# Products of constants on PE inside the layer norm blocks of a twelve-sublayer transformer kernel

## The chip, the cores and the metric

The kernel runs on one core of a Trainium2 chip. The metric is device time in microseconds (us) of one execution. The engines are named as in the profile: PE (TensorE, its matmuls), PEld (TensorE's weight loads), DVE (VectorE), ACT (ScalarE), POOL (GpSimd) and SP (SyncE, which only issues DMAs here). PE's granted clock has two levels, 1.2 and 2.4 GHz, which the profile writes as 0.50 and 1.00.

## The reference

Four layers of three sublayers each (cross attention, self attention, feed forward) on x of 16 x 64 rows of 256 numbers, in float32. Each sublayer is added to x and begins with a layer norm of x:

```python
def _layernorm(x, axis=-1, eps=1e-05):
    m = jnp.mean(x, axis=axis, keepdims=True)
    v = jnp.var(x, axis=axis, keepdims=True)
    return (x - m) / jnp.sqrt(v + eps)
...
x = x + _L0_xattn_ref(_layernorm(x, axis=-1), ctx_1024, ctx_1024, ...)
x = x + _L0_attn_ref(_layernorm(x, axis=-1), ...)
x = x + _L0_ffn_ref(_layernorm(x, axis=-1), ...)
...
x = x + _L3_ffn_ref(_layernorm(x, axis=-1), ...)
```

So there are twelve of these norms. The cross attentions also read a context of 16 x 1601 rows of 256.

## The kernel before, in words

x stays in SBUF as 8 tiles (`T`) of 128 rows by 256 columns. `build` runs the twelve sublayers one after the other, each as a chain of blocks. A block gives each engine its own program; engines wait for each other by semaphores, the block ends when every engine's program has ended, and the helper `signals` (line 39) then clears the semaphores and puts a barrier of all engines behind it. So the next block starts when the slowest engine of this one has finished, SP's wait for its loads included.

Each sublayer begins with the helper `layernorm` (line 83). The twelve calls are, in order of time: `x0_ln` (line 573), `e0_in` (736), `f0_ln` (1199), `s1_ln` (1443), `a1_ln` (2214), `g1_ln` (2385), `x2_ln` (3633), `a2_ln` (3671), `f2_ln` (3976), `x3_ln` (4125), `a3_ln` (4350) and `q3_ln` (4415). In the texts they go by their first two letters: x0, e0, f0 and so on. Ten of them hand over `env.h_T`, in which the normed rows are wanted turned (features on the partitions); e0 and q3 hand over None and turn nothing.

Inside `layernorm`:

- DVE measures the 8 tiles (line 105) and gathers mean and variance per half of 4 tiles (line 110). ACT takes the square root (line 142), DVE inverts (line 115).
- ACT norms the 4 tiles of the first half (line 150), DVE those of the second half (line 129).
- PE turns each tile by two transposes of 128 x 128 (line 167) against the identity `env.ident`, 16 in all. It waits for each tile of the first half from ACT and for each of the second from DVE. The turned first half goes to PSUM banks 0 and 1, the second to 2 and 3.
- When a half is turned, ACT copies its one bank to `h_T` (line 155) and DVE its other (line 134). The semaphore `turned` tells them.
- SP issues the loads that the sublayer wants (line 72) and waits for them; those in `begun` (line 96, used by e0 and g1) are waited for only by who reads them.

The order on PE and in every queue is the order of the code; nothing is scheduled by a tool. What follows a norm differs: x0, x2, x3 go on with `linear_T` (line 265); s1 with 8 products at line 1457; a1 at line 2014; g1 at line 2458; a2 at line 3723; f0 and f2 with the experts' products at line 471, whose weights SP begins to load only in that next block (line 446); a3 with a small product at line 4376 whose input is loaded in the next block (line 4369).

`env.ident` is the first 128 columns of the tile `consts`, which is loaded once at the start and holds zeros, ones and some masks; it is wider than 512 columns. PSUM has 8 banks of 512 float32 columns; the norm uses banks 0 to 3.

Of the kernel before, what the change touches and what calls it, by code (L numbers as in the profile page):

```python
# [17 lines left out]
P = 128  # L18
# [6 lines left out]
NH = 512  # L25
# [57 lines left out]
def layernorm(nc, env, stage, src, nat, dst_T, loads=(), begun=(), begun_in=None):  # L83


    HALF = T // 2
    with signals(nc, stage, "loaded own stats std shift_ready rows_act rows_dve turned act_out "
                 "dve_out") as (
            loaded, own, stats, std_ready, shift_ready, rows_act, rows_dve, turned, act_out,
            dve_out):  # L90
        with nc.Block() as block:

            @block.sync
            def _(sp):
                for dst, src_rows in begun:
                    sp.dma_start(dst, src_rows).then_inc(begun_in, 16)
                load_all(sp, loads, loaded)

            @block.vector
            def _(dve):  # L100
                steps = Steps(dve, own)

                def measure(tiles):
                    for t in tiles:
                        steps.done(nc.vector.bn_stats(env.bn[:, t, :], src[:, t, :]))

                def aggregate(half):
                    steps.wait()
                    for t in range(HALF * half, HALF * (half + 1)):
                        nc.vector.bn_aggr(env.mv[:, t, :], env.bn[:, t, :]).then_inc(stats, 1)  # L110

                def invert(half):
                    ts = slice(HALF * half, HALF * (half + 1))
                    dve.wait_ge(std_ready, half + 1)
                    steps.done(nc.vector.reciprocal(env.rstd[:, ts], env.std[:, ts]))
                    steps.wait()

                measure(range(HALF))
                aggregate(0)
                measure(range(HALF, HALF + 1))  # L120
                invert(0)
                nc.vector.scalar_tensor_tensor(
                    out=env.shift[:, :], in0=env.mv[:, 0:HALF, 0], scalar=-1.0,
                    in1=env.rstd[:, 0:HALF], op0=ALU.mult, op1=ALU.mult).then_inc(shift_ready, 1)
                measure(range(HALF + 1, T))
                aggregate(1)
                invert(1)
                for t in range(HALF, T):
                    nc.vector.tensor_scalar(nat[:, t, :], src[:, t, :], env.mv[:, t, 0:1],
                                            env.rstd[:, t:t + 1], ALU.subtract,  # L130
                                            ALU.mult).then_inc(rows_dve, 1)
                for half in range(2 if dst_T is not None else 0):
                    dve.wait_ge(turned, 2 * half + 2)
                    nc.vector.tensor_copy(dst_T[:, 1, half * NH:(half + 1) * NH],
                                          env.ps[:, 2 * half + 1, :]).then_inc(dve_out, 1)

            @block.scalar
            def _(act):
                def deviations(half):
                    ts = slice(HALF * half, HALF * (half + 1))  # L140
                    act.wait_ge(stats, HALF * (half + 1))
                    nc.scalar.activation(env.std[:, ts], env.mv[:, ts, 1], ACT.Sqrt,
                                         bias=env.eps5[:, 0:1]).then_inc(std_ready, 1)

                deviations(0)
                act.wait_ge(shift_ready, 1)
                for t in range(HALF):
                    if t == HALF - 1:
                        deviations(1)
                    nc.scalar.activation(nat[:, t, :], src[:, t, :], ACT.Identity,  # L150
                                         scale=env.rstd[:, t:t + 1], bias=env.shift[:, t:t + 1]
                                         ).then_inc(rows_act, 1)
                for half in range(2 if dst_T is not None else 0):
                    act.wait_ge(turned, 2 * half + 1)
                    nc.scalar.copy(dst_T[:, 0, half * NH:(half + 1) * NH],
                                   env.ps[:, 2 * half, :]).then_inc(act_out, 1)

            @block.tensor
            def _(pe):
                for t in range(T if dst_T is not None else 0):  # L160
                    half, at = t // HALF, t % HALF * P
                    if half == 0:
                        pe.wait_ge(rows_act, t + 1)
                    else:
                        pe.wait_ge(rows_dve, t - HALF + 1)
                    for f in range(KT):
                        last = nc.tensor.transpose(env.ps[:, 2 * half + f, at:at + P],
                                                   nat[:, t, f * P:(f + 1) * P], env.ident)
                        if t % HALF == HALF - 1:
                            last.then_inc(turned, 1)  # L170

# [4358 lines left out]
def build(nc, d, out, where, names):  # L4532
    with ExitStack() as mem:
        def sb(name, shape, dt=F32):
            return mem.enter_context(nc.sbuf_tensor(name, shape, dt))

        env = Env()
        env.x = sb("x", [P, T, D])
        env.h = sb("h", [P, T, D])
        env.h_T = sb("h_T", [P, KT, N])  # L4540
        env.rows = sb("rows", [P, T, D])
        env.bn, env.mv = sb("bn", [P, T, 6]), sb("mv", [P, T, 2])
        env.std, env.rstd = sb("std", [P, T]), sb("rstd", [P, T])
        env.shift = sb("shift", [P, T // 2])
        consts = sb("consts", [P, d["consts"].shape[1]])
        env.ident = consts[:, where["ident"][0]:where["ident"][1]]
        env.ones = consts[:, where["ones"][0]:where["ones"][1]]
        env.same_head = consts[:, where["same_head"][0]:where["same_head"][1]]
        env.den_rows = consts[:, where["den_rows"][0]:where["den_rows"][1]]
        env.head_of = consts[:, where["head_of"][0]:where["head_of"][1]]  # L4550
        env.excluded = consts[:, where["excluded"][0]:where["excluded"][1]]
        env.parity = consts[:, where["parity"][0]:where["parity"][1]]
        env.iota8 = consts[:, where["iota8"][0]:where["iota8"][1]]
        env.valid_last = consts[:, where["valid_last"][0]:where["valid_last"][1]]
        env.cross = consts[:, where["cross"][0]:where["cross"][1]]
        env.own_state = consts[:, where["own_state"][0]:where["own_state"][1]]
        env.tenth = consts[:, where["tenth"][0]:where["tenth"][1]]
        env.block_of = consts[:, where["block_of"][0]:where["block_of"][1]]
        env.zero = consts[:, where["zero"][0]:where["zero"][1]]
        env.eps5 = consts[:, where["eps5"][0]:where["eps5"][1]]  # L4560
        env.eps6 = consts[:, where["eps6"][0]:where["eps6"][1]]
        env.minus1 = consts[:, where["minus1"][0]:where["minus1"][1]]
        env.state_mask = consts[:, where["same_head"][0]:where["head_of"][1]]
        env.ps = mem.enter_context(nc.psum_tensor("ps", [P, 8, NH], F32))

        with signals(nc, "start", "x_in consts_in") as (x_in, consts_in):
            with nc.Block() as block:

                @block.sync
                def _(sp):  # L4570
                    sp.dma_start(env.x[:, :, :], d["x"].rearrange("(t b) s n -> (b s) t n", b=2)
                                 ).then_inc(x_in, 16)
                    sp.dma_start(consts[:, :], d["consts"]).then_inc(consts_in, 16)
                    sp.wait_ge(x_in, 16)
                    sp.wait_ge(consts_in, 16)

        for name in names:
            SUBLAYERS[name](nc, env, d)

        with signals(nc, "end", "stored") as (stored,):  # L4580
            with nc.Block() as block:

                @block.sync
                def _(sp):
                    sp.dma_start(out.rearrange("(t b) s n -> (b s) t n", b=2), env.x[:, :, :]
                                 ).then_inc(stored, 16)
                    sp.wait_ge(stored, 16)
# [96 lines left out]
```

## Time and profile before

| what | value |
|---|---|
| time, median of 3 runs | 3715.51 us (3709.92 to 3716.82) |
| the profiled execution's own time | 3718.34 us |
| its span in the trace | 3716.5 us |
| mean granted clock of PE | 0.952 |
| PE busy | 3395.4 us, 91% of the span, 39440 products |
| DVE, ACT, POOL busy | 2017.8, 1690.3, 701.8 us |

The profiled execution took 3718.34 us, of which 3716.5 us lie inside the trace's span and 1.8 us around it. All times of rows are from the span's start. "Idle before" in a row of the timeline is how long the engine had done nothing when the work of that row began, and the name behind the arrow is what it waited for; "PEq" there stands for the queue of instructions itself, which is what a barrier between two blocks looks like. A matmul's record lasts from its start to its modelled end, so the records of successive products overlap; how far apart they start is what each costs in a row of them.

### The profile page before, as it was taken

How to read it: one execution, taken by the hardware profiler on the slowest of the kernel's cores; microseconds unless marked ns; L12 is line 12 of the kernel's file. 1: busy time of each engine (PE TensorE's matmuls, PEld its weight loads, DVE VectorE, ACT ScalarE, POOL GpSimd, SP SyncE). 2: the span in 40 equal slices, each digit the busy share in tenths (PEclk: the TensorE clock that was granted, in tenths of full speed). 3: DMA queues.
4: the chain of work that ended last, by engine and by line, in shares of the span. 5: the costliest groups of instructions: out<-in, count | busy, mean ns of one | idle time of the engine just before them, and what ended most of it. 6: DMA issues, size and time to landing. Idle time of an engine off the chain costs nothing. (4 is left out here: it accounts for less than half of the span.)

```text
span 3716.5 us, 90513 instructions
## 1 busy us (share of the span) xinstructions
PE 3395.4 (91%) x39440; PEld 2395.7 (64%) x39440; DVE 2017.8 (54%) x4042; ACT 1690.3 (45%) x3093; POOL 701.8 (19%) x343
## 2 busy tenths in 40 slices
PE   6999999779998979999879998999999789998975
PEld 4777777656675668888654455777776555554544
DVE  4666666654443267777546483565656443333337
ACT  3777777523332277887535452444444321111222
POOL 1776777311010000000122021101010000000001
PEclk8999999989999989999978998999999889999986
DMA  1111111021001415334010002111110013220710
GB/s 64 55 38 38 38 55 38 10 92 38 27 1 60 155 47 195 127 127 151 16 51 1 1 0 69 59 40 59 40 50 11 24 38 110 92 75 3 253 43 16
DMA packets 155253, 223.53 MB, mean 60 GB/s; under 512 B 39375, under 2 KB 134539, under 8 KB 154732
## 3 DMA queue, kind: packets, MB, share of 16 engines
q1 hardware_dynamic: 154860, 217.75, 17.6%
q8 instruction: 313, 5.13, 0.6%
q14 instruction: 80, 0.66, 0.1%
HBM read 216.67 MB, written 1.05 MB: 59 GB/s over the span
## 5 line engine op out<-in xcount | busy, mean ns | idle before, releaser
L3225 POOL TENSOR_TENSOR x_sc<-x_sc,h_T 128x2048 f32<-128x2048 f32 (+1 forms) x105 | 443.4, 4267 | 200.3 <-ACT h_T L3438 200.3
L3041 ACT ACTIVATE x_sc<-x_sc,x_nb 128x2048 f32<-128x2048 f32 (+1 forms) x112 | 210.6, 1880 | 297.6 <-DVE x_sc L3090 297.5
L3090 DVE SCALAR_TENSOR_TENSOR x_sc<-ps,x_nb,x_cap 128x2048 f32<-128x2048 f32 (+1 forms) x112 | 246.2, 2198 | 49.4 <-PE ps L2982 49.4
L3513 DVE TENSOR_TENSOR x_most<-x_most,ps 128x512 f32<-128x512 f32 (+1 forms) x352 | 234.8, 685 | 45.5 <-PE ps L3342 33.1
L1736 ACT ACTIVATE s1i_both<-ps,s_less,s_rs_s 128x64 f32<-128x64 f32 x624 | 215.2, 426 | 49.0 <-DVE s_less L1853 48.9
L3417 ACT COPY x_sc<-ps 128x1024 f32<-128x1024 f32 x192 | 179.4, 945 | 112.0 <-PE ps L3342 71.5
L3431 ACT ACTIVATE x_sc<-x_sc 128x2048 f32<-128x2048 f32 (+1 forms) x112 | 201.0, 1797 | 4.0 <-DVE x_sc L3225 3.9
L3298 PE MATMUL ps<-x_wv,x_ctx_T 128*128 128x256 f32 (+1 forms) x832 | 201.4, 383 | 0.0
L2953 PE MATMUL ps<-x_ctx_T,x_wk 128*128 128x401 f32 (+1 forms) x512 | 200.0, 517 | 1.5 <-PEq L44 1.5
L3290 PE MATMUL ps<-x_ctx_T,x_wk 128*128 128x401 f32 (+1 forms) x512 | 197.3, 523 | 4.0 <-POOL x_v L3254 3.4
L2961 PE MATMUL ps<-x_wv,x_ctx_T 128*128 128x256 f32 (+1 forms) x832 | 197.7, 379 | 0.0
L2961 PEld LDWEIGHTS ps<-x_wv,x_ctx_T 128*128 128x128 f32 (+1 forms) x832 | 154.3, 185 | 51.5 <-issue 3.2
L3074 DVE COPY x_v<-ps 128x512 f32<-128x512 f32 (+1 forms) x112 | 73.0, 652 | 208.4 <-PE ps L2961 208.4
L508 ACT ACTIVATE f_hid_T<-ps 128x512 f32<-128x512 f32 x68 | 40.6, 597 | 303.8 <-PE ps L471 303.8
L3298 PEld LDWEIGHTS ps<-x_wv,x_ctx_T 128*128 128x128 f32 (+1 forms) x832 | 150.4, 186 | 39.8 <-issue 3.0
L1630 PE MATMUL ps<-s_q,s1i_ctx_T 128*64 128x64 f32 x4992 | 159.2, 225 | 10.3 <-DVE s_q L1816 8.1
L1630 PEld LDWEIGHTS ps<-s_q,s1i_ctx_T 128*64 128x64 f32 x4992 | 154.8, 140 | 19.3 <-DVE s_q L1816 9.9
L1668 PE MATMUL ps<-s1i_ctx_n,s1i_both 128*64 128x257 f32 x1248 | 148.6, 388 | 8.2 <-DVE s1i_both L1873 8.2
L533 DVE SCALAR_TENSOR_TENSOR x<-ps,f_comb,x 128x256 f32<-128x256 f32 x192 | 83.9, 479 | 131.9 <-PE ps L486 131.9
L524 DVE TENSOR_TENSOR f_hid_T<-f_hid_T,ps 128x512 f32<-128x512 f32 x68 | 46.8, 688 | 191.2 <-PE ps L471 191.2
L2574 PE MATMUL ps<-g_ew,g_hm 128*128 128x512 f32 (+1 forms) x384 | 145.0, 532 | 0.0
L3359 PE MATMUL ps<-x_sc,x_v 128*17 128x64 f32 x6656 | 118.0, 222 | 23.6 <-ACT x_sc L3431 21.4
(518 smaller groups left out, 6837.9 us busy)
## 6 DMA issues: line engine op xcount, KB each, us to landing
x_ctx_T<-in_ctx_T SPq DMA_DIRECT2D x32, 1601.0 KB
s1i_ctx_T<-in_ctx_T SPq DMA_DIRECT2D x16, 1601.0 KB, 8.1
x3i_ctx_T<-in_ctx_T SPq DMA_DIRECT2D x16, 1601.0 KB, 7.3
s1i_ctx_n<-in_ctx SPq DMA_DIRECT2D x16, 1536.0 KB
x3i_ctx_n<-in_ctx SPq DMA_DIRECT2D x16, 768.0 KB
h<-in_ctx SPq DMA_DIRECT2D x12, 896.0 KB
e_w<-in_L_attn_W SPq DMA_DIRECT2D x8, 1024.0 KB, 6.9
rows<-in_ctx SPq DMA_DIRECT2D x12, 640.0 KB
```

What stands on the lines that cost most here:

```text
L1630: last = nc.tensor.matmul(ps[side * S:(side + 1) * S, 2 * b + c, at:at + S], ctx_T[lane][:, b, k, keys], q2[lane][:, k, b * S:(b + 1) * S] ...
L1736: nc.scalar.activation(att[lane][:, b, t, :], ps[:, 2 * b + c, at:at + S], ACT.Exp, scale=rs_s[lane][:, b, t:t + 1], bias=less[lane][:, b, ...
L2953: last = nc.tensor.matmul(ps[:, bank, 0:width], w_k[:, k, m * P:(m + 1) * P], ctx_T[row % 2][:, k, at:at + width], start=(k == 0), stop=(k ...
L2961: last = nc.tensor.matmul(ps[0:keys, bank, j * D:(j + 1) * D], ctx_T[row % 2][:, k, t * P:t * P + keys], w_v[:, k, :], start=(k == 0), sto ...
L3041: nc.scalar.activation(x, x, ACT.Square, scale=DH ** -0.5, bias=nb[0:keys, 0:1]).then_inc(squared, 1)
L3090: nc.vector.scalar_tensor_tensor(out=slot[0:keys].rearrange("p r m h j q -> p (r m h) (j q)")[:, :, 0:width], in0=score_banks[0:keys].rear ...
L3225: return eng.tensor_tensor(x, x, most_of, ALU.subtract)
L3290: last = nc.tensor.matmul(ps[:, bank, 0:width], w_k[:, k, m * P:(m + 1) * P], ctx_T[row % 2][:, k, at:at + width], start=(k == 0), stop=(k ...
L3298: last = nc.tensor.matmul(ps[0:keys, bank, j * D:(j + 1) * D], ctx_T[row % 2][:, k, t * P:t * P + keys], w_v[:, k, :], start=(k == 0), sto ...
L3417: nc.scalar.copy(x[0:keys, rs].rearrange("p r h j q -> p r h (j q)")[:, :, :, 0:width], score_banks[0:keys, rs].rearrange("p r h j q -> p ...
L3431: nc.scalar.activation(x, x, ACT.Exp, scale=DH ** -0.5).then_inc(exped, 1)
L3513: ins = nc.vector.tensor_tensor(best[0:keys, rs], best[0:keys, rs], score_banks[0:keys, rs, :, j, :], ALU.max)
```

## The change

In each norm's block PE gets products of its own: the identity against the first 512 columns of `consts`, into bank 7, which nothing reads. Where rows are turned there are two of them before the first turn, one between the first half's turns and the second's, and one behind the last. In e0 and q3, where nothing is turned, there are four. That is 10 x 4 + 2 x 4 = 48 products of 128 x 128 by 512 columns. They wait for nothing and signal nothing.

```diff
@@ layernorm
     HALF = T // 2
+    SPARE_BANK = 7
+    BUSY_AHEAD = 2 if dst_T is not None else 4
...
             @block.tensor
             def _(pe):
+                def keep_busy(n):
+                    for _ in range(n):
+                        nc.tensor.matmul(env.ps[:, SPARE_BANK, :], env.ident,
+                                         env.consts[:, 0:NH], start=True, stop=True)
+
+                keep_busy(BUSY_AHEAD)
                 for t in range(T if dst_T is not None else 0):
...
                         if t % HALF == HALF - 1:
                             last.then_inc(turned, 1)
+                    if t % HALF == HALF - 1:
+                        keep_busy(1)
...
@@ build
-        consts = sb("consts", [P, d["consts"].shape[1]])
+        consts = env.consts = sb("consts", [P, d["consts"].shape[1]])
```

On PE, from the end of the experts of f0 through the norm s1 to the products of the next block, the program before reads (`x16` counts the instructions of a row, the names are those of the tiles written and read):

```order
L486 MATMUL ps<-f_w,f_hid_T 128x256 x16
L437 UNCONDITIONAL_BRANCH
L158 UNCONDITIONAL_BRANCH
L167 MATMUL ps<-consts,h 128x128 x16
L91 UNCONDITIONAL_BRANCH
L1452 UNCONDITIONAL_BRANCH
L1457 MATMUL ps<-s1i_both 128x256 x4
```

and with the change (line 164 is the new product, line 175 the turn):

```order
L496 MATMUL ps<-f_w,f_hid_T 128x256 x16
L447 UNCONDITIONAL_BRANCH
L160 UNCONDITIONAL_BRANCH
L164 MATMUL ps<-consts 128x512 x2
L175 MATMUL ps<-consts,h 128x128 x8
L164 MATMUL ps<-consts 128x512
L175 MATMUL ps<-consts,h 128x128 x8
L164 MATMUL ps<-consts 128x512
L93 UNCONDITIONAL_BRANCH
L1462 UNCONDITIONAL_BRANCH
L1467 MATMUL ps<-s1i_both 128x256 x4
```

The third product stands between the first half's signal and the second half's turns, the fourth behind the signal of the last turn. At e0, whose norm had nothing on PE, the program now reads:

```order
L164 MATMUL ps<-consts 128x512 x4
L93 UNCONDITIONAL_BRANCH
L813 UNCONDITIONAL_BRANCH
L827 MATMUL ps<-consts,h 128x128 x16
```

Here four products stand alone before the barrier and the next block. The other engines and SP keep their programs as they were.

## Rows read from the trace of the kernel before

**Rows 1.** The page: busy time of the engines, and PE's clock in 40 slices.

```profile
PE 3395.4 (91%) x39440; PEld 2395.7 (64%) x39440; DVE 2017.8 (54%) x4042; ACT 1690.3 (45%) x3093; POOL 701.8 (19%) x343
...
PEclk8999999989999989999978998999999889999986
```

**Rows 2.** Timeline, the norm s1: start us, us, engine, line, work [idle before].

```profile
1307.86 1.41 DVE L105 BATCH_NORM_STATS2 bn<-x 128x6 f32<-128x256 f32 x4 [0.82 <-PEq L44]
...
1311.11 4.06 PE L167 MATMUL ps<-consts,h 128*128 128x128 f32 x16 [4.98 <-ACT h L150]
...
1312.47 1.38 DVE L129 TENSOR_SCALAR h<-x,mv,rstd 128x256 f32<-128x256 f32 x4
...
1315.20 0.69 DVE L134 COPY h_T<-ps 128x512 f32<-128x512 f32 x1 [0.75 <-PE ps L167]
```

**Rows 3.** One line's instructions, duration in ns min/median/max: turns, and x0's products of 512.

```profile
L167 PE MATMUL ps<-consts,h x160: 272/421/478, 13.5 to 3583.4; 128*128 128x128 f32 x160
...
L265 PE MATMUL ps<-h_T,x_sc x16: 592/592/1192, 21.8 to 30.9; 128*128 128x512 f32 x16
```

**Rows 4.** Stretches of x0's products: busy us (count) by engine, PEclk, DMA, GB/s.

```profile
21.80:27.00 5.20, 5.17 (x6) 2.19 (x7) 0.00 (x0) 0.69 (x1) 0.00 (x0) 0.50 0.00 0
27.10:31.00 3.90, 3.90 (x11) 1.65 (x9) 0.69 (x1) 0.69 (x1) 0.00 (x0) 1.00 0.00 0
```

**Rows 5.** Timeline of PE: the first products behind the norms, with PE's idle time before them.

```profile
21.83 9.66 PE L265 MATMUL ps<-h_T,x_sc 128*128 128x512 f32 x16 [4.59 <-PEq L44]
...
756.89 1.33 PE L817 MATMUL ps<-consts,h 128*128 128x128 f32 x5 [18.66 <-DVE h L1009]
...
1182.97 4.64 PE L471 MATMUL ps<-h_T,f_w 128*128 128x512 f32 x5 [5.17 <-DMA f_w<-in_L_ffn_W]
...
1316.67 3.75 PE L1457 MATMUL ps<-s1i_both 128*128 128x256 f32 x8 [1.50 <-PEq L44]
...
1929.18 4.53 PE L2458 MATMUL ps<-h_T,g_rw 128*64 128x512 f32 x5 [2.91 <-DMA g_sel<-in_expert_sel]
...
2260.20 4.61 PE L265 MATMUL ps<-h_T,x_wq 128*128 128x512 f32 x5 [5.69 <-PEq L44]
...
2921.57 2.04 PE L3723 MATMUL ps<-a_wv,h_T 128*128 128x256 f32 x4 [3.84 <-PEq L44]
...
3592.71 4.53 PE L4376 MATMUL ps<-a_rel_bd,a_onehot 128*128 128x64 f32 x20 [8.92 <-DMA a_rel_bd<-in_L_attn_rel_emb]
```

**Rows 6.** Timeline, the first DMA issue of the block behind f0's norm.

```profile
1179.26 0.40 SPq L446 DMA_DIRECT2D f_w<-in_L_ffn_W  x1
```

**Rows 7.** Stretches in and behind norms: f0 (first two), s1, a1, g1, x3, columns as Rows 4.

```profile
1174.10:1177.20 3.10, 3.07 (x13) 2.28 (x14) 2.59 (x12) 2.23 (x5) 0.00 (x0) 0.50 0.00 0
1177.30:1178.50 1.20, 0.50 (x5) 0.26 (x3) 0.84 (x2) 0.59 (x1) 0.00 (x0) 1.00 0.00 0
1316.60:1320.40 3.80, 3.73 (x9) 3.05 (x10) 0.33 (x2) 0.00 (x0) 0.13 (x1) 0.50 0.01 2
1320.50:1324.00 3.50, 3.50 (x11) 1.90 (x11) 0.69 (x1) 0.98 (x2) 0.00 (x0) 0.98 0.00 0
...
1844.60:1848.50 3.90, 3.89 (x9) 1.80 (x10) 0.34 (x2) 1.45 (x2) 3.90 (x2) 1.00 0.02 6
...
1929.10:1935.00 5.90, 5.82 (x7) 1.67 (x8) 0.00 (x0) 1.97 (x2) 5.45 (x5) 0.50 0.59 188
1935.10:1938.00 2.90, 2.90 (x8) 1.16 (x7) 0.00 (x0) 1.02 (x2) 0.00 (x0) 1.00 0.83 303
...
3397.60:3401.50 3.90, 3.87 (x9) 1.82 (x10) 0.16 (x1) 0.69 (x1) 0.00 (x0) 1.00 0.00 0
```

**Rows 8.** In the sublayer x3: PE's timeline around a gap, and a stretch behind it.

```profile
3422.73 1.09 PE L4215 MATMUL ps<-consts,x3i_ctx_T 128*128 128x128 f32 x8
3426.04 2.36 PE L4215 MATMUL ps<-consts,x3i_ctx_T 128*128 128x128 f32 x11 [2.22 <-DVE x_ctx_t L4332]
...
3426.70:3430.00 3.30, 3.30 (x15) 2.65 (x16) 2.38 (x4) 0.41 (x2) 0.00 (x0) 0.50 0.00 0
```

## The prediction

> **What bounds the kernel now.** I read the page first. PE is busy 91% of the span and DVE 54%, and PE's granted clock is near full except in a few slices [rows 1]. So whatever delays PE, or makes it run at 1.2 instead of 2.4 GHz, is paid; what happens on the other engines mostly isn't. The change touches PE only, in twelve short blocks of 7 to 11 us. So I read next the timeline of one of them, s1, then the price of a product, then what PE waits for behind each norm, then the clock in and behind the norms.
>
> In s1 [rows 2] DVE begins at 1307.86 and PE has its first turn at 1311.11, after 4.98 us of idleness, waiting for ACT's first normed tile. The 16 turns last 4.06 us. DVE's last copy, at 1315.20 and 0.69 long, is what ends the block at 1315.89. The next block's first product begins at 1316.67, and PE sat idle 1.50 us before it [rows 5]: the copy and the barrier. That 1.50 us is what a norm shows whose end waits for nothing but its own work. Behind x0, x2 and a2 the idle time is 4.59, 5.69 and 3.84 us [rows 5]: there SP still waits for the sublayer's loads after the copies are done (x2 has one more small block besides, but over 3 us are left). Behind a3 it is 8.92 us, against 5.17 behind f0, where the same steps follow (copy, barrier, a load issued in the next block, its landing) and the block's end is not late: f0's next load is issued at 1179.26, and the turns ended at 1182.97 - 5.17 = 1177.80, so 1.46 us lie between, as in s1 [rows 5, 6]. So a3 has 3.7 us of slack too. g1's next product waits for a load issued inside the norm, 2.91 us, which leaves 2.91 - 1.50 = 1.4 us of slack. Tight are five: f0 and f2 (built alike), s1, a1 and x3 (the last two with the 1.50 us of s1).
>
> **The price of a product.** x0's products have the new one's shape. At clock 0.50 six take 5.17 us, 0.86 us each; at 1.00 it is half, 0.43 (nine weight loads in 3.9 us) [rows 4]. From start to end one takes 0.59 us at full clock, and 1.19 at most [rows 3]. A turn of 128 columns is a quarter: 0.21 us at 0.50.
>
> **The change, part by part.**
>
> *The products ahead.* Two take at most 2 x 0.86 = 1.7 us from the block's start, and the first turn comes 3.25 us after DVE's start [rows 2]. Cost 0; the cover is the 4.98 us of idleness, and without it each would cost 0.86. The four in e0 and q3 take at most 3.4 us; PE has been idle for 18.66 us when e0's next block wants it [rows 5], and q3's is built alike. Cost 0.
>
> *The product between the halves.* The first half is signalled before it, so its copies don't wait. Behind it in PE's queue stand the eight turns of the second half, and behind them DVE's copy, the block's end and every engine. DVE's normed tiles start at 1312.47, some 0.35 us apart [rows 2], so at 0.50 PE is the late one: the product delays the turns by its whole 0.86 us. At full clock it is 0.43.
>
> *The product behind.* The last turn's record ends at 1311.11 + 4.06 = 1315.17; such a record lasts 0.42 [rows 3], so it begins at 1314.75, and the product at 1314.96. It ends 1.06 to 1.19 us later, at 1316.0 to 1316.15, where DVE's copy ends at 1315.89. So 0.13 to 0.26 us at clock 0.50, and nothing at full clock, where 0.59 us lie well inside the copy. I take 0.13.
>
> *What that makes.* A tight norm at clock 0.50 pays 0.86 + 0.13 = 0.99 us; one where the clock rises within the turns, as in f0, where it is 0.50 until 1177.2 and 1.00 from 1177.3 [rows 7], pays about 0.5. I take three of the one and two of the other: 3 x 0.99 + 2 x 0.5 = **+4.0 us** (ends: 5 x 0.43 = 2.2 and 5 x 1.12 = 5.6). x0, x2, a2, a3 and g1 pay nothing: 0.99 is below the slack of each.
>
> *What comes back.* Behind s1's norm PE works 3.8 us at 0.50 before it gets 1.00, behind g1's 5.9 us [rows 7]. Had the clock been full, half of that would go: 1.9 and 2.9 us. In f0 the clock rose just before the end of the turns, with nothing but turns before it [rows 7]; a1 and x3 go into the next block at 1.00 already [rows 7]. So behind about 4 us of turns the clock was up in some norms and not in others. With both products PE's work grows to about 4.06 + 0.86 + 0.86 = 5.8 us, near g1's 5.9 us before its rise, the longest of these stretches. So I take it that s1 and g1 go into their next block at 1.00: **-1.9 - 2.9 = -4.8 us**. Whether a clock once up lasts over the barrier is shown by a1 and x3, with 1.50 us of idleness. For a1 and x3 themselves 0; for x0, f0, x2, f2, a3 also 0, because PE is idle 4.6 us or more afterwards and comes back at 0.50, as x0 does today [rows 4, 5]. a2 lies between (3.84 us less 0.86): bounds 0 and, by s1's row, -1.9; I take 0.
>
> TensorE: Matmul & The Clock Gate (the Trainium skill, Part 4, PE-mode transpose) says that transposes don't count as busy time for the clock as products do, and that it stays low. This trace doesn't agree: f0's clock rose on turns alone [rows 7]. By that rule the turns would add nothing to the four products, nothing would come back, and the sum would be that of the first rival.
>
> **The sum** is +4.0 - 4.8 = -0.8 us. Against the profiled execution's own 3718.34 us that is 3717.5; that execution lies 2.8 us above the median of 3715.51, and the median becomes **3714.7 us**. A measurement of this kernel can tell about 0.2% from no change, 7.4 us: the three times before lie 6.9 us apart. Bounds of the terms alone: +2.2 - 6.7 = -4.5 and +5.6 + 0 = +5.6.
>
> **The rivals.**
>
> *The products raise no clock.* They only stand in the way: 5 x 0.99 = +5.0, 3720.5 us. For it: s1, g1 and x0 need 3.8 to 5.9 us of unbroken products before the clock rises, and the norm's work has gaps between its first turns. Against: the turns alone do it in f0. Chance 0.18.
>
> *The products ahead keep the clock up through the whole norm.* Then all turns run at full clock, wait only for DVE's tiles, and end at about 1312.47 + 1.38 + 0.4 = 1314.3 instead of 1315.17: -0.9 in each of five norms, with the middle product hidden in the waits; and s1, g1 and a2 get their 1.9, 2.9 and 1.9 us. Together -11.2, 3704.3 us. Against it stand rows of x3: eight turns (1.09 us, the size of two products at full clock), then 2.22 us of idleness, and the next 3.3 us of PE ran at 0.50 [rows 8]. Between the products ahead and the first turn lie 1.5 to 2.4 us of the same kind, and 1.5 us or more before them. Chance 0.13.
> The Trainium skill's page TensorE: Matmul & The Clock Gate (Why this matters for your kernels) advises to avoid long idle gaps between bursts of matmuls, and by that rule short bursts in the gap would hold the clock. The rows of x3 speak against it.
>
> *Slower: a1 and x3 lose the full clock they have.* Their turns happened to end so that the clock had just risen; with the middle product the turns end 0.86 us later, and if products don't help the clock, both may go on at 0.50. Price 1.9 us each, by s1's row, beside the 5.0 of the first rival: 5.0 + 3.8 = +8.8, 3724.3 us. It decides only if both fall: with one it is +6.9, which is still no difference. For it: the rise is a matter of moment in this trace, s1 and g1 not having it in time. Against: more work on PE should not make it come later. Chance 0.08.
>
> That the change doesn't do what it says can be left out: the 48 products stand in PE's program, and nothing but the block's end waits for them.
>
> **How the numbers follow.** Forecast 0.61 (its own range 3711 to 3719), no clock raised 0.18, clock kept up 0.13, a1 and x3 fall 0.08. The first two are within 0.2% but for a small tail, the others outside: faster 0.15, same 0.77, slower 0.08. The range takes the forecast and the first rival with the scatter of the median of a few runs, and part of the way to the others: 3706 to 3721.
>
> **What would show it.** The middle and last product each once in ten norms, 0.86 us at clock 0.50; PE's idle time before the next block's product in s1, a1 and x3 shorter, since its own product fills it; the copies' end 0.5 to 0.9 us later after DVE's start than the 8.03 us of s1; the stretch behind s1 and g1 at clock 1.00; no change behind x0, x2, a3, e0 and q3. The forecast is wrong if the first turns run at 1.00 (then it is faster), or if s1, g1, a1 and x3 go on at 0.50 (then it is slower).

## The result, and the profile after

Over 20 runs each the changed kernel took 3713.8 us (3705.48 to 3727.64) and the kernel before 3722.57 us. The ratio, estimated from the single runs, is 0.9981, with a 95% interval of 0.9973 to 0.9989: 7 us less, between 4 and 10 (the two medians lie 8.8 us apart). Measured once more, on the same chip as two of the experiments below, it came to 0.9971 (0.9960 to 0.9981). The median of the kernel before is 7 us higher than that of the three runs shown ahead of the prediction, so the predicted time was met (3714.7), while the predicted change was not: -0.8 us against some -7 to -11. That the time came out within 1 us is luck: the base moved up by nearly as much as the change was mis-sized.

The page of the changed kernel, as Rows 1 showed it before:

```profile
PE 3423.0 (92%) x39536; PEld 2401.1 (65%) x39536; DVE 2017.6 (54%) x4042; ACT 1688.8 (46%) x3093; POOL 702.4 (19%) x343
...
PEclk8999999989999999999988999999999989999987
```

PE has 27.6 us more of busy time than before [rows 1] in a span that is 12.8 us shorter (3703.7 against 3716.5; both executions are single ones and their kernels scatter by several us). And it has 96 matmul records more, where the program has 48 more products. The answers on the new line and on the turns say the same:

```profile
L164 PE MATMUL ps<-consts x96: 592/596/1193, 10.4 to 3674.5; 128*128 128x512 f32 x96
...
L175 PE MATMUL ps<-consts,h x160: 272/273/478, 13.9 to 3571.2; 128*128 128x128 f32 x160
```

One product of float32 in the program is two matmul instructions on the chip, a turn is one. So each product costs 0.86 us at full clock (x3 below, 3383.75 to 3384.61) and 1.71 at 0.50 (e2 below, 1310.91 to 1312.62), twice what the prediction priced. The line of the turns shows the second thing: the median record fell from 421 to 273 ns [rows 3], so more than half of the turns now run at full clock (there a record lasts under 350 ns, at 0.50 it lasts 410 or more).

PE's timeline of the norm s1 and of what follows, the counterpart of [rows 2, 5]:

```profile
1305.91 1.95 PE L164 MATMUL ps<-consts 128*128 128x512 f32 x4 [1.73 <-PEq L44]
1309.16 1.42 PE L175 MATMUL ps<-consts,h 128*128 128x128 f32 x6 [1.29 <-ACT h L152]
1310.82 0.44 PE L175 MATMUL ps<-consts,h 128*128 128x128 f32 x2 [0.24 <-ACT h L152]
1311.10 1.83 PE L164 MATMUL ps<-consts 128*128 128x512 f32 x2
1312.71 1.92 PE L175 MATMUL ps<-consts,h 128*128 128x128 f32 x8
1314.42 1.11 PE L164 MATMUL ps<-consts 128*128 128x512 f32 x2
1316.29 1.97 PE L1467 MATMUL ps<-s1i_both 128*128 128x256 f32 x8 [0.75 <-PEq L44]
```

and DVE's first and last instruction in it:

```profile
1305.91 1.41 DVE L107 BATCH_NORM_STATS2 bn<-x 128x6 f32<-128x256 f32 x4 [0.82 <-PEq L44]
...
1314.67 0.69 DVE L136 COPY h_T<-ps 128x512 f32<-128x512 f32 x1 [2.16 <-PE ps L175]
```

The first turns run at full clock. Then the clock falls within the middle product, which takes 1.6 us (1311.10 to the turn at 1312.71), and the eight turns behind it run at half speed. From DVE's start to the end of its copy it is 1315.36 - 1305.91 = 9.45 us, where it was 8.03: 1.4 us lost in the norm. But the eight products of the next block take 1.97 us, where they took 3.75 [rows 5]: the clock has come back behind the last turns.

In x3 the clock holds all through:

```profile
3378.57 1.96 PE L164 MATMUL ps<-consts 128*128 128x512 f32 x4 [1.72 <-PEq L44]
3381.82 1.42 PE L175 MATMUL ps<-consts,h 128*128 128x128 f32 x6 [1.29 <-ACT h L152]
3383.48 0.44 PE L175 MATMUL ps<-consts,h 128*128 128x128 f32 x2 [0.24 <-ACT h L152]
3383.75 1.02 PE L164 MATMUL ps<-consts 128*128 128x512 f32 x2
3384.61 1.04 PE L175 MATMUL ps<-consts,h 128*128 128x128 f32 x8
3385.49 1.02 PE L164 MATMUL ps<-consts 128*128 128x512 f32 x2
3387.26 2.38 PE L275 MATMUL ps<-h_T,x3i_wq 128*128 128x512 f32 x5 [0.75 <-PEq L44]
```

There DVE's copy ends 7.81 us after its start, 0.15 us earlier than before (7.96) although a product of 0.86 us stands in the path: eight turns take 0.9 us and not 1.7. Of the ten norms that turn, seven end their copies at 7.8 to 7.95 us and three (s1, g1, a2) at 9.4 to 9.5; before all lay at 7.65 to 8.04. The norms as such have therefore become no shorter. The gain is behind them, as four stretches show (f0, s1, g1, a2; columns as Rows 4):

```profile
1183.20:1187.20 4.00, 3.94 (x13) 2.03 (x13) 0.00 (x0) 0.89 (x2) 0.00 (x0) 1.00 0.91 271
1316.30:1320.00 3.70, 3.70 (x13) 2.54 (x14) 0.98 (x3) 1.02 (x2) 0.07 (x1) 1.00 0.01 2
1924.00:1930.00 6.00, 5.99 (x14) 2.24 (x15) 0.00 (x0) 2.95 (x4) 5.71 (x6) 1.00 0.48 126
2911.60:2914.00 2.40, 2.37 (x8) 1.44 (x8) 0.42 (x1) 0.00 (x0) 2.38 (x4) 1.00 0.00 0
```

All four are at 1.00, where the kernel before had 0.50 for 3.3 to 5.9 us: s1 and g1 in [rows 7], f0 and a2 here:

```profile
1182.90:1187.50 4.60, 4.53 (x6) 1.95 (x7) 0.00 (x0) 0.69 (x1) 0.00 (x0) 0.50 1.01 315
2921.50:2925.00 3.50, 3.43 (x6) 2.17 (x7) 0.42 (x1) 0.00 (x0) 3.44 (x5) 0.52 0.00 0
```

Halving those stretches would give 2.2 (f0), 1.9 (s1), 2.9 (g1) and 1.7 us (a2).

These places don't explain the whole difference of the two traces. Counted from DVE's start in one norm to its start in the next, the stretches from f0, s1, g1 and a2 on are shorter by 2.7, 1.3, 4.1 and 1.0 us, together 9.1 of the 12.8. From a1 on it is 2.1 us and from x3 on 1.7, though neither norm changed by more than 0.2 us and both blocks behind them were at 1.00 before too. From a1 on the trace of e5, which has no product in these norms, is shorter by 2.0 us as well, so that part is scatter of the single execution.

### The profile page after: what moved, and what is told of

The parts are those of the page before. It is cut to its first block and busy times, and to the rows that moved or that the text cites. A ratio compares the mean times of both kernels' runs of the same rounds, so it can differ in the third digit from the quotient of the medians.

```text
span 3703.7 us, 90705 instructions
## 1 busy us (share of the span) xinstructions
PE 3423.0 (92%) x39536; PEld 2401.1 (65%) x39536; DVE 2017.6 (54%) x4042; ACT 1688.8 (46%) x3093; POOL 702.4 (19%) x343
```

## The experiments

Each ratio is to the kernel before on the same chip, estimated from 5 to 12 single runs against 18 to 35, so it need not be the quotient of the medians; "us below" is worked out from the ratio. e1 to e4 ran on one chip, e5 to e8 on a second, e9 to e11 on a third. "Cold" means at clock 0.50. "Copies' end" is the time from DVE's start in a norm to the end of its last copy, which is what a product on the path moves.

**e1: only the products ahead.**

```diff
-                        keep_busy(1)
+                        keep_busy(0 if half == 0 else 0)
```

> Only the products ahead are kept (2 per turning norm, 4 in e0 and q3), those between the halves and behind the last turn are gone. Theory A (the products ahead bring or hold PE's clock before the turns, and the turns then keep it up): most of the gain stays and the delay of about 1.4 us in norms with a cold middle product goes, so 7 to 11 us below the kernel before, first turns at clock 1.00 in most norms, copies ending 7.8 to 8.0 us after DVE's start. Theory B (what raises the clock is the longer unbroken work of turns and the products between and behind): the turns run as before, 0.50 in most norms, and the time is within 2 us of the kernel before.

Measured 3713.28 us, ratio 0.9973 (0.9962 to 0.9983), 10 us below. The norm s1:

```profile
1304.75 1.95 PE L164 MATMUL ps<-consts 128*128 128x512 f32 x4 [1.74 <-PEq L44]
1308.00 1.42 PE L175 MATMUL ps<-consts,h 128*128 128x128 f32 x6 [1.29 <-ACT h L152]
1309.66 1.58 PE L175 MATMUL ps<-consts,h 128*128 128x128 f32 x10 [0.24 <-ACT h L152]
1312.74 1.97 PE L1467 MATMUL ps<-s1i_both 128*128 128x256 f32 x8 [1.50 <-PEq L44]
```

Copies end 7.22 us after DVE's start (s1: 8.03 before, 0.8 more) in eight of the ten norms, and the second half's turns are at 1.00 in eight. That is theory A. g1 still went on at 0.50 for 6 us, for its wait of 2.48 us on a load; x3 too, in this execution. The products ahead alone give what the whole change gives.

**e2: only the products between and behind.**

```diff
-    BUSY_AHEAD = 2 if dst_T is not None else 4
+    BUSY_AHEAD = 0
```

> Only the products between the halves and behind the last turn are kept, none ahead. Theory A: the turns of the first half run at 0.50, the middle product is cold and costs up to 1.7 us; the next block begins at 1.00 more often. Five tight norms pay up to 1.7 us each, s1, g1 and a2 get 2 to 3 us back: between 3 us below and 4 us above the kernel before. Theory B: the whole gain stays, 6 to 9 us below the kernel before.

Measured 3716.14 us, ratio 0.9985 (0.9976 to 0.9994), 6 us below: more than theory A gave it, though the interval, 2 to 9 us, reaches into both expectations. In s1:

```profile
1308.77 2.35 PE L175 MATMUL ps<-consts,h 128*128 128x128 f32 x8 [4.97 <-ACT h L152]
1310.91 1.91 PE L164 MATMUL ps<-consts 128*128 128x512 f32 x2
1312.62 1.92 PE L175 MATMUL ps<-consts,h 128*128 128x128 f32 x8
1314.33 1.33 PE L164 MATMUL ps<-consts 128*128 128x512 f32 x2
1316.41 1.97 PE L1467 MATMUL ps<-s1i_both 128*128 128x256 f32 x8 [0.75 <-PEq L44]
```

Here the first half's turns are cold in all ten norms (copies' end 8.5 to 9.7 us, so up to 1.7 us lost in each), but the next block starts at 1.00 in s1, a1, g1 and x3 alike. So there are two gains: the products ahead make the turns fast, the others carry the full clock into the next block. Both theories are right about one half each.

All the traces together say it more firmly than one. Behind s1 and g1 the next block began at 1.00 in all nine traces of kernels with a product behind the turns; in the four without (before, e1, e5, e6) it did so in two behind s1 and in none behind g1. And the eight turns of the first half all ran at full clock in none of the 50 norms without a full-width product ahead, in 30 of 60 with two of them, and in 18 of 20 with three.

**e3: all products, half as wide.**

```diff
-                        nc.tensor.matmul(env.ps[:, SPARE_BANK, :], env.ident,
-                                         env.consts[:, 0:NH], start=True, stop=True)
+                        nc.tensor.matmul(env.ps[:, SPARE_BANK, 0:NH // 2], env.ident,
+                                         env.consts[:, 0:NH // 2], start=True, stop=True)
```

> As the changed kernel, but each product is 256 columns wide, so that it costs what my prediction priced a product of 512 at: 0.43 us at full clock, 0.86 at 0.50. If the step that failed is this price (the trace shows each product twice, 0.86 and 1.71 us), the prediction's sum should come true here: 1 us below the kernel before, within 3, cold norms with copies ending 0.9 us later than before, and first turns at 0.50 in most norms. If the price does not matter to the clock: 6 to 9 us below, as the changed kernel.

Measured 3713.7 us, ratio 0.9982 (0.9971 to 0.9992), 7 us below, between 3 and 11. So the sum, 1 us below, did not come true although every price did; only the interval's edge reaches into the 3 us to either side that it was given. In s1 the middle product takes 0.85 us and the turns are cold:

```profile
1307.31 1.10 PE L164 MATMUL ps<-consts 128*128 128x256 f32 x4 [1.73 <-PEq L44]
1310.55 2.35 PE L175 MATMUL ps<-consts,h 128*128 128x128 f32 x8 [2.14 <-ACT h L152]
1312.70 1.06 PE L164 MATMUL ps<-consts 128*128 128x256 f32 x2
1313.55 1.91 PE L175 MATMUL ps<-consts,h 128*128 128x128 f32 x8
```

Copies end at 8.85 to 8.89 us in seven norms, the 0.86 us of the prediction over 8.03. s1, a1, g1 and x3 all go on at 1.00, which is the return that the prediction counted. x0 and f0 begin at 1.00 too, but lose it after 0.5 and 0.2 us and then run at 0.50 for 3.4 us, where it was 5.1 and 4.5 in the kernel before: a part of the return that the prediction put at 0. The rest of the 7 us was not traced to a place, and the profiled execution lies only 4.3 us under that of before.

**e4: no product between the halves.**

```diff
-                        keep_busy(1)
+                        keep_busy(0 if half == 0 else 1)
```

> As the changed kernel without the product between the halves. Theory A: as the changed kernel in the clock, less the delay where the middle product was cold (s1 1.4, others hidden): 1 to 4 us below the changed kernel, copies ending at most 8.0 us after DVE's start in s1, g1 and a2. Theory B: the clock is up less often behind the norms (s1 and g1 at 0.50 in the next block, 2 to 3 us each), so 1 to 4 us above the changed kernel.

Measured 3710.69 us, ratio 0.9969 (0.9957 to 0.9981): 11.5 us below. The copies' end is at 7.2 us in five norms and 7.5 to 8.0 in the others, and s1, a1, g1 and x3 go on at 1.00. So fast turns, as in e1, and the full clock behind them, as in e2, stand in one trace, without the product in the path. Against the changed kernel the intervals overlap, so the time alone does not choose between the two theories; the traces show the difference per norm (0.6 us where both are at full clock, 7.81 and 7.21).

**e5: products in e0 and q3 alone.**

```diff
-    BUSY_AHEAD = 2 if dst_T is not None else 4
+    BUSY_AHEAD = 0 if dst_T is not None else 4
...
-                        keep_busy(1)
+                        keep_busy(0 if half == 0 else 0)
```

> Products only in e0 and q3 (four each), none in the ten norms that turn. Theory A (the gain comes from PE's clock in the turning norms and just behind them): no change, ratio 0.999 to 1.001. Rival theory C (the gain is not of the norms' clock: any added products shift PE's clock elsewhere, or the e0 and q3 products matter): 3 us or more below the kernel before, ratio under 0.999.

Measured 3720.61 us, ratio 0.9999 (0.9990 to 1.0009). Those eight products do nothing that a time could show (the interval is some 4 us to either side), and these additions do not by themselves shift the kernel: theory C falls.

**e6: only the products ahead, half as wide.**

```diff
-                        nc.tensor.matmul(env.ps[:, SPARE_BANK, :], env.ident,
-                                         env.consts[:, 0:NH], start=True, stop=True)
+                        nc.tensor.matmul(env.ps[:, SPARE_BANK, 0:NH // 2], env.ident,
+                                         env.consts[:, 0:NH // 2], start=True, stop=True)
...
-                        keep_busy(1)
+                        keep_busy(0 if half == 0 else 0)
```

> Products ahead only, and 256 columns wide, so two of them are the 0.86 us at full clock (1.71 at 0.50) that my prediction took for two of 512. Theory A with the price as the failed step: so short a burst does not hold the clock, the first turns are at 0.50 in most norms that come in at full clock, and the time is within 3 us of the kernel before, against 10 below with the full width. If the price is not what decides: 7 to 11 us below, as with the full width.

Measured 3717.05 us, ratio 0.9987 (0.9976 to 0.9998): 5 us below, with an interval of 1 to 9 us that holds neither expectation off. The trace is clearer. In x3:

```profile
3382.61 1.10 PE L164 MATMUL ps<-consts 128*128 128x256 f32 x4 [1.72 <-PEq L44]
3385.85 4.06 PE L175 MATMUL ps<-consts,h 128*128 128x128 f32 x16 [2.14 <-ACT h L152]
```

PE came in at full clock as in x3 above, but with half the work ahead and 2.14 us idle instead of 1.29 the turns took the 4.06 us of [rows 2]. The copies' end is 8.03 to 8.04 us in nine norms of ten, and the second half's turns were cold in all of them; in a2 the last one was fast (7.90). So the products ahead hold the clock at their real size and not at the size that the prediction gave them. Halving them changed two things at once, the work and the idle time behind it; which of the two decides is not shown. What the 5 us are, if they are not scatter, stays open.

**e7: three ahead, none between, one behind.**

```diff
-    BUSY_AHEAD = 2 if dst_T is not None else 4
+    BUSY_AHEAD = 3 if dst_T is not None else 4
...
-                        keep_busy(1)
+                        keep_busy(0 if half == 0 else 1)
```

> Three products ahead instead of two, none between the halves, one behind. Three take 2.6 us at full clock, which fits ahead of the first turn, and 5.1 us at 0.50, which does not (the first turn comes 3.25 us after DVE's start): where PE comes in at 0.50 (f0, f2, x2) the turns start up to 1.9 us late, where it comes in at 1.00 the gap to the first turn shrinks from 1.3 to about 0.4 us and the clock always holds. Theory A: within 2 us of the kernel with two ahead and one behind (11 below the kernel before). Theory B (the work behind counts): no gain over it, and slower by the late turns, 1 to 3 us.

Measured 3707.62 us (3707.32 to 3709.62), ratio 0.9965 (0.9952 to 0.9978), 13 us below: as e4 within the intervals, and within 2 us of theory A's 11. Copies end at 7.21 us in eight norms. f2 comes in at 0.50 and shows what a burst that is too long costs:

```profile
3010.51 5.46 PE L164 MATMUL ps<-consts 128*128 128x512 f32 x6 [1.42 <-PEq L44]
3015.76 2.31 PE L175 MATMUL ps<-consts,h 128*128 128x128 f32 x16
```

The first turn comes 5.25 us after the block's start and not 3.25, and yet the copies end at 8.30 us, 0.3 later than before, for the turns then wait for nobody and the clock rises in them.

**e8: products wherever PE waits for loads.** With the e4 kernel as base:

```diff
-                        keep_busy(0 if half == 0 else 1)
+                        keep_busy(0 if half == 0 else {"x0_ln": 3, "x2_ln": 3, "a2_ln": 2}.get(stage, 1))
...
@@ run_experts, PE's program
+                for _ in range(3):
+                    nc.tensor.matmul(env.ps[:, 7, :], env.ident, env.consts[:, 0:NH],
+                                     start=True, stop=True)
                 for item in plan.seq:
```

> As the kernel with two ahead and one behind, with more products where PE waits for loads: three behind x0's and x2's turns, two behind a2's, and three at the head of the experts' blocks of f0 and f2, where PE waits for the first weights for 3.7 us. Theory A: the clock is full when x0, f0, a2 and f2 go on, which saves half of the 5.2, 4.5, 3.4 and 3.3 us that the kernel before spends at 0.50 there: 4 to 8 us below the kernel with two ahead and one behind, ratio to the kernel before 0.995 to 0.996. Where the clock is at 0.50 when these products are issued they are late by up to 2 us each place and the gain shrinks to 0.

Measured 3701.69 us (3691.13 to 3708.85), ratio 0.9951 (0.9937 to 0.9965), 18 us below the kernel before. By the ratios that is 7 below e4, which ran on another chip, and 5 below e7 on the same one; the intervals overlap in either case. The profiled execution is the fastest of the six, 3691.13 us. x0, the first of [rows 5]:

```profile
16.73 2.74 PE L164 MATMUL ps<-consts 128*128 128x512 f32 x6
21.53 2.38 PE L275 MATMUL ps<-h_T,x_sc 128*128 128x512 f32 x5 [2.07 <-PEq L44]
```

The stretch behind it, against the 0.50 and the six records of [rows 4]:

```profile
21.50:27.00 5.50, 5.47 (x13) 2.58 (x14) 0.69 (x1) 0.73 (x2) 0.00 (x0) 1.00 0.00 0
```

x2 and f2 went on at 1.00 without a fall within 12 us, f0 nearly so; a2 did not; its next block began 1.2 us later there than in the trace of before (12.34 against 11.14 us from DVE's start), but without its extra products it began as late in e4 (12.04) and e11 (12.64). The five places were changed together, so what each gives was not measured. x0 is the least sure: its next block ran at 1.00 in e2 and e10 too, which have one product behind, and in e9, which has three, it began at 0.50.

**e9: the same with three ahead.**

```diff
-    BUSY_AHEAD = 2 if dst_T is not None else 4
+    BUSY_AHEAD = 3 if dst_T is not None else 4
```

> The bridging kernel with three products ahead instead of two. Theory A: the clock is full for the turns in all norms that come in at full clock, also where two ahead lost it (a1, g1), copies ending 7.2 us after DVE's start; the two norms that come in at 0.50 (f0, f2) may start their turns up to 1.9 us late. 0 to 4 us below the bridging kernel with two ahead, ratio to the kernel before 0.994 to 0.9955.

Measured 3697.49 us (3695.73 to 3699.63, 5 runs), ratio 0.9936 (0.9924 to 0.9949): 24 us below the kernel before, the best of all. Against e8, on another chip, it is 6 us by the ratios, with overlapping intervals. All 16 turns are at full clock in all ten norms, and the copies end at 7.2 us in seven, 7.65 to 7.9 in x0, f0 and f2.

**e10: two products between the halves.**

```diff
-                        keep_busy(1)
+                        keep_busy(2 if half == 0 else 1)
```

> The changed kernel with two products between the halves instead of one: the price of a product on the path. At full clock one more costs 0.86 us in each norm, of which nothing is hidden any more, at 0.50 1.71 us (my prediction's price would be 0.43 and 0.86). Five tight norms, and g1 with what is over its slack: copies end 0.86 to 1.71 us later after DVE's start than with one, 8.7 us where it was 7.81, and the time is 4 to 7 us above the changed kernel, about that of the kernel before. By my prediction's price: 2 to 4 us above.

Measured 3711.91 us, ratio 0.9974 (0.9964 to 0.9983). In s1:

```profile
1309.54 1.88 PE L164 MATMUL ps<-consts 128*128 128x512 f32 x4
1311.26 1.04 PE L175 MATMUL ps<-consts,h 128*128 128x128 f32 x8
```

The copies' end is 8.67 us in eight norms, 0.86 more than the 7.81 of one product at full clock: the price is as measured on the line. The total isn't: it lies 1 us above the changed kernel of the same call and not 4 to 7. The intervals, some 4 us to either side, would just allow the lower end. In the traces the changed kernel has norms at 9.3 to 9.5 us where the clock fell in the middle (three in one execution, three in the other), this one has two (9.26 and 10.36). So it seems to win back part of its price by keeping the clock, but that part was not isolated.

**e11: the changed kernel again.**

> The changed kernel once more, on the same chip as the other two, as the mark that they are compared with: 5 to 9 us below the kernel before (ratio 0.9975 to 0.9987), if the first measurement of 0.9981 holds.

Measured 3710.89 us, ratio 0.9971 (0.9960 to 0.9981): slightly more than the first time, with overlapping intervals. In this execution x3, which held the clock in the trace above, lost it in the middle (copies' end 9.49 us), and s1 held it (7.81). Which norm falls is a matter of the single execution, and that is part of the kernel's scatter.

## Why the prediction was right, and where it was not

- **That PE's clock in and behind the norms is what counts** held. e5 leaves out the ten norms and gains nothing; e1, e2 and e4 gain with the products there.
- **"x0's products have the new one's shape ... 0.86 us each"** failed, by a factor of two. The shape is right; but a product in the program is two instructions, and the prediction divided x0's stretch by instructions. It could be read beforehand: the order of the program has s1's products as 128x256 x4 where [rows 5] has x8. The middle product costs 0.86 us, as e10 shows (7.81 to 8.67), to 1.71, as e2 does, not 0.43 to 0.86.
- **"The products ahead: cost 0"** held with two: where they ran at 0.50 the first turn came 0.2 to 0.3 us late (x0, x2, f2), and the copies there ended at 7.81 to 7.95 us as elsewhere. But their use was put at 0 too, in the forecast, and that was the larger failure. The rival that has them keep the clock up gave -0.9 us per norm; e1 shows -0.8 (8.03 to 7.22). It was turned down by rows in which 1.09 us of work and a gap of 2.22 us lost the clock [rows 8]. With the right price the burst is 1.95 us and the gap 1.29, so those rows said nothing on it. They did say what e6 showed, where the burst is 1.10 and the gap 2.14.
- **The delay by the middle product, +4.0 us** was right in kind. In the changed kernel it is hidden where the clock holds (7.81 against 8.03, the fast turns pay for it) and is 1.4 us where the clock falls. Summed over the five tight norms of that trace the copies ended 1.1 us later (f0 +0.16, s1 +1.42, a1 -0.11, f2 -0.22, x3 -0.15), not 4.0: the fast turns, which the sum did not have, more than made up for the doubled price. In e2, without the products ahead, the same sum is 5.9 us. e3, with the size that was priced, shows exactly the 0.86.
- **The product behind, put at nothing at full clock,** was off by 0.1: the next block begins 0.88 us after the copies' end in x3, against 0.77 in the kernel before, since two instructions outlast the copy.
- **What comes back, -4.8 us from s1 and g1**, held for those two. "0" for f0 and a2 did not in this trace: the idle time of f0 is 3.69 us and that of a2 1.67, where it was 5.17 and 3.84, and both go on at 1.00. But these two are draws. In e11 f0 went on at 1.00 again and a2 at 0.50, after 4.70 us of idleness; of the nine traces with a product behind the turns a2 went on at 1.00 in two. And s1's return is counted against a trace in which s1 had lost the clock: in e5, whose norm is that of the kernel before, it went on at 1.00. "0" for a1 and x3 was read off one execution, in which they happened to be at 1.00. The execution at hand lay 4 us under the later median of the kernel before. Others of it may lose there what s1 lost, as x3 did in e1, but no trace of the kernel before itself shows it. How often they fall in the kernel before can't be said from single traces.
- **The rival that the products raise no clock** fell by e1 to e4. **The slower one** fell too: a1 and x3 kept the full clock in the changed kernel, both times.
- **In short:** the forecast's two effects are real, a delay on the path and a return behind the norms, but a product was priced at half, and a third effect, that of the products ahead on the turns, was put at nothing. The path was to lose 4.0 us and lost 1.1 in the trace; and 4.0 us came back behind f0 and a2, put at 0, beside the 4.8. That gives 1.1 - 4.8 - 4.0 = -7.7 us, near the measured -7; as f0 and a2 are draws, the nearness should not be leaned on.
- **TensorE: Matmul & The Clock Gate** (the Trainium skill, Part 4, PE-mode transpose) has transposes not count for the clock. e5 speaks against it once more, for these float32 turns: no norm that turns has a product there, yet the last three turns of s1 were fast and its next block began at 1.00, behind turns alone. Its advice to avoid long idle gaps between bursts (Why this matters for your kernels) was the better guide: e8 follows it where PE waits for loads and came out 5 to 7 us lower than e7 and e4, with intervals that overlap.

## What to carry to other kernels

Before pricing an added operation, count the instructions that it becomes: a float32 product of the program was two on the chip, and the count in the trace against the count in the program says so. Where an engine waits anyway, idle work of the right length can pay for itself through the clock (in this kernel 0.2 to 0.6% of the time); put it ahead of the wait's end and behind the block's last work, not between two steps of the path. And read a clock effect from several executions or from many like places, since one trace shows only one draw of it.

## What the hardware showed that was not expected

A burst of constants that nobody reads can keep PE's clock up over a wait: with 1.95 us of products, 1.73 us idle before and 1.29 after them, the following turns ran at 1.00 (s1 and x3), while 1.10 us of products with 2.14 us behind lost it in the same places (e6). It is not sure with two products: the whole first half was fast in 30 of 60 norms, and in e8 a1 had not one fast turn. With three it was fast in 18 of 20. The whole kernel gained 24 us of 3721 in e9 with PE doing some 37 us more of busy work (3432.6 against 3395.4). The full clock also outlasted 3.69 us of idleness behind f0's norm, which was longer than gaps over which it was lost elsewhere (2.22 us in [rows 8], 1.50 behind x3 in e1).
